# Cross attention with latents: the steps of all engines ordered by due times, and the mask's additive row made on VectorE

## The reference, cut to what matters

```python
x   = _layernorm(features, gm, bm)          # context, 16 x 128 x 256
lat = _layernorm(latents, gl, bl)           # latents, 16 x 128 x 256, normalised once more before this
kv_input = jnp.concatenate([x, lat], axis=1)                      # 256 rows
q, k, v = lat @ Wq, kv_input @ Wk, kv_input @ Wv                  # 16 heads of 64
sim = einsum('bhqd,bhfd->bhqf', q * SCALE, k)
sim = where(kv_mask, sim - max(sim), -inf)                        # mask over the 128 context rows only
out = einsum('bhqf,bhfd->bhqd', softmax(sim), v) @ Wo             # added to the activations
```

## Time and profile before

| what | value |
|---|---|
| median of 3 runs | 4432.84 us (4424.89 to 4438.37) |
| the profiled execution's own time | 4435.27 us |
| its span | 4433.8 us |
| busy over the span | PE 74%, DVE 56%, ACT 37%, POOL 32% |
| the stage | 2047.9 to 2777.9 us, 730 us |
| in the stage (2047 to 2785) | PE busy 602.4 us, DVE 240.8, ACT 258.2, POOL 137.1; mean granted clock 0.96 |

### The profile page before, as it was taken

One profiled execution on the slowest core, in us unless ns is written; L12 is line 12 of the kernel. 1 busy time (PEld: TensorE's weight loads), 2 busy tenths in 40 slices (PEclk: granted clock), 3 DMA queues, 4 the chain that ended last, 5 costly groups with the idle time before them and its releaser, 6 DMA issues. The chain is left out here.

```text
span 4433.8 us, 52962 instructions
## 1 busy us (share of the span) xinstructions
PE 3279.0 (74%) x17693; PEld 2111.6 (48%) x17693; DVE 2479.3 (56%) x6511; ACT 1624.7 (37%) x3647; POOL 1407.1 (32%) x1086
## 2 busy tenths in 40 slices
PE   5988887867925677766888888466679666767698
PEld 3666665646612233223566656345456422335555
DVE  6878784364336888885323323535442278855443
ACT  3666654111204544542333334224302144424311
POOL 4666664103452444452212212200010245520010
PEclk7888887888967888888999999679869778989899
DMA  2000000302430000000000000110021200000000
GB/s 89 5 9 6 9 8 9 124 20 82 127 111 39 0 0 0 0 0 14 7 1 1 1 1 1 37 78 1 13 101 29 74 0 1 0 27 1 1 1 20
DMA packets 71034, 116.12 MB, mean 26 GB/s; under 512 B 28689, under 2 KB 58537, under 8 KB 68018
## 3 DMA queue, kind: packets, MB, share of 16 engines
q1 hardware_dynamic: 61170, 86.50, 5.8%
q0 software_dynamic: 9600, 26.23, 2.4%
HBM read 88.58 MB, written 24.12 MB: 25 GB/s over the span
## 5 line engine op out<-in xcount | busy, mean ns | idle before, releaser
L1224 POOL TENSOR_TENSOR L_attn_state<-L_attn_state,L_attn_ccol 128x1024 f32<-128x1024 f32 x192 | 452.3, 2356 | 527.5 <-DVE L_attn_state L1217 526.1
L1217 DVE TENSOR_TENSOR_SCAN L_attn_state<-L_attn_decay,bank 128x1024 f32<-128x1024 f32 x192 | 438.3, 2283 | 41.1 <-ACT L_attn_decay L1194 15.3
L1183 PE MATMUL bank<-L_attn_state,ident 128*128 128x512 f32 x768 | 421.2, 678 | 19.4 <-POOL L_attn_state L1224 19.3
L1177 PE MATMUL bank<-L_attn_parts,L_attn_select 96*128 96x512 bf16 x384 | 137.9, 441 | 256.7 <-DVE bank L1209 241.8
L1194 ACT ACTIVATE L_attn_decay<-L_attn_dt,L_attn_A 128x512 f32<-128x512 f32 x384 | 256.2, 716 | 129.3 <-DVE L_attn_state L1217 116.3
L1103 POOL TENSOR_TENSOR L_xattn_prob<-L_xattn_prob,L_xattn_inv 128x1024 f32<-128x1024 f32 x64 | 121.2, 1895 | 567.2 <-DVE L_xattn_inv L1086 567.2
L1209 DVE TENSOR_TENSOR bank<-L_attn_dtx,bank 128x1024 f32<-128x1024 f32 x192 | 236.0, 1229 | 57.0 <-PE bank L1177 50.7
L1183 PEld LDWEIGHTS bank<-L_attn_state,ident 128*128 128x128 f32 x768 | 164.7, 217 | 185.4 <-issue 129.9
L1177 PEld LDWEIGHTS bank<-L_attn_parts,L_attn_select 96*128 96x128 bf16 x384 | 29.9, 102 | 391.0 <-DVE bank L1209 340.0
L736 ACT ACTIVATE L_xattn_prob<-bank,L_xattn_top 128x128 f32<-128x128 f32 x512 | 135.8, 416 | 195.9 <-DVE L_xattn_top L778 195.9
L1027 ACT ACTIVATE L_xattn_prob<-L_xattn_masked,L_xattn_low 128x256 f32<-128x256 f32 x256 | 127.0, 497 | 209.2 <-DVE L_xattn_low L1081 127.3
(11 more groups left out here) (601 smaller groups left out, 7705.4 us busy)
## 6 DMA issues: line engine op xcount, KB each, us to landing
L_ffn_ew<-in_L_ffn_experts SPq DMA_DIRECT2D x4, 3072.0 KB, 21.2
L_ffn_made<-L_ffn_yout SPq DMA_DIRECT2D x24, 512.0 KB, 3.0
L_ffn_w<-in_L_ffn_w SPq DMA_DIRECT2D x4, 2048.0 KB, 14.6
L_xattn_ctx<-in_ctx_rows SPq DMA_DIRECT2D x3, 2048.0 KB, 8.2
L_ffn_rows<-L_ffn_xh SPq DMA_DIRECT2D x8, 512.0 KB, 2.9
L_ffn_made<-L_ffn_yout SPq DMA_DIRECT2D x12, 256.0 KB, 2.1
L_attn_rows<-in_x SPq DMA_DIRECT2D x16, 128.0 KB, 6.9
turned<-L_attn_rows SPq DMA_DIRECT2D x16, 128.0 KB, 2.3
```

The costliest lines, as they stand in the source:

```text
L1177: pe.matmul(self.spread.bank(2 * N + i)[:, :], self.select[:, NSTATE * i + n, :], parts[:, :], start=True, stop=True).then_inc(*self.sprea ...
L1183: t = pe.matmul(self.y[unit % len(self.y)][m][:, :], self.c.ident[:, :], self.state[N % 3][:, m, :], start=n == 0, stop=n == 15)
L1217: dve.tensor_tensor_scan(flat(self.state[N % 3]), flat(self.decay[N % 2]), flat(self.drive), 0.0, ALU.mult, ALU.add).then_inc(*self.scanne ...
L1224: pool.tensor_tensor(state[:, :, :], state[:, :, :], self.ccol[N % 2][:, :].unsqueeze(1).broadcast_to([P, 2, GT]), ALU.mult).then_inc(*sel ...
```

## The change

In words:

- The order comes from three tables of due times, in units of a quarter of a sequence: one for steps that come once (or twice) per unit, one for those of a sequence (period 4), one for those of a group of four sequences (period 16). All steps are sorted by their time.
- Filling a bank and copying it out are now steps of their own (q and qcopy, k and kcopy, v and vcopy, flip and flipped, turn and turned, mix and unmix, out and add), so the copy can have another place in its engine's list than the fill in TensorE's.
- low and exp are split by bank (j = 0, 1), with two signals `softened` per unit.
- The norms and the first q and k of sequence 0 are written out in front.
- The mask's weights are loaded onto all 128 partitions (the DMA's source repeats the row). Per sequence one DVE instruction makes `hidden` from them (step hidden). The step hide, its fill of the side bank, its copy, the cast, the tile `hide` and TensorE's wait at the beginning are gone. DVE does the memset of `hidden` alone at the start.
- As copies have places of their own, two waits are new: qcopy waits until the scores of sequence a-2 were filled, and hidden until they were emptied. The banks, what fills them and who empties which are as before.

The core of the diff:

```diff
+LATENTS_BY_UNIT = {"score": -0.06, "low": (-0.06, 0.72), "exp": (0.58, 1.11), "invert": 1.37, "flip": (2.15, 2.29), "flipped": (2.31, 2.4),
+                   "mix": 2.61}
+LATENTS_BY_SEQUENCE = {"turn": -2.96, "turned": -2.96, "q": (-2.57, -1.04), "qcopy": (-2.42, -1.18), "kcopy": (-2.38, -1.34, -0.67, -0.54),
+                       "k": (-2.11, -1.46, -0.78, -0.67), "hidden": -0.49, "vcopy": (-0.37, 0.17, 0.49, 0.81), "v": (-0.35, 0.07, 0.39, 0.64),
+                       "unmix": (4.77, 6.27), "out": 6.63, "add": 6.89}
+LATENTS_BY_GROUP = {"stats_other": -11.44, "stats_outer": -6.96, "apply_outer": -5.74, "apply_other": -4.85, "stats_inner": -3.89,
+                    "apply_inner": -3.38}
...
+def due_by(table, period, turns):
+    for kind, at in table.items():
+        each = at if isinstance(at, tuple) else (at,)
+        yield from ((period * turn + time, kind, len(each) * turn + i) for turn in turns for i, time in enumerate(each))
...
     def order():
         yield "begin", 0
-        yield from norms(0)
-        yield from front(0)
...
+        for step in LATENTS_BY_GROUP:
+            yield step, 0
+        yield "hidden", 0
+        for what, copied, times in (("turn", "turned", 1), ("q", "qcopy", 2), ("k", "kcopy", 4)):
+            for n in range(times):
+                yield what, n
+                yield copied, n
+        first = ("hidden", "turn", "turned", "q", "qcopy", "k", "kcopy")
+        due = chain(due_by(LATENTS_BY_UNIT, 1, range(UNITS)), due_by(LATENTS_BY_SEQUENCE, 4, range(NSEQ)), due_by(LATENTS_BY_GROUP, 16, range(1, NGROUP)))
+        yield from as_due([(time, kind, n) for time, kind, n in due if kind not in first or n >= {"q": 2, "qcopy": 2, "k": 4, "kcopy": 4}.get(kind, 1)])
...
-        elif what == "hide":
-            at = side[what, n]
-            dve.wait_ge(*side.filled(at))
-            dve.tensor_copy(hidden[n % 2][:, 0:P], side.bank(at)[:, 0:P]).then_inc(*side.done(at))
+        elif what == "hidden":
+            if n >= 2:
+                dve.wait_ge(*score[1].emptied(4 * (n - 2) + 3))
+            else:
+                dve.wait_ge(*cleared.at(0))
+            dve.tensor_scalar(hidden[n % 2][:, 0:P], w["keep"][:, n * P:(n + 1) * P], 0.0, 1e30, ALU.is_equal, ALU.mult).then_inc(*hid.up())
...
+        elif what == "exp":
+            i, j = divmod(n, 2)
+            if i >= 3 and j == 0:
+                act.wait_ge(*flip.filled(2 * (i - 3) + 1))
+            act.wait_ge(*score[j].emptied(i))
+            for h in (j, 2 + j):
+                t = act.activation(prob[i % 3][:, h, :], masked[i % 2][:, h, :], ACT.Exp, bias=low[:, i % 2, h:h + 1], scale=-1.0,
+                                   accum_out=total[:, i % 3, h:h + 1])
             t.then_inc(*softened.up())
```

More of the change, by code:

```diff
@@ L52, in __init__ @@
         self.gone = {e: s.flag(f"{name}_emptied_{e}") for e in sorted(set(by))}
+        self.latest = {}
     def bank(self, n):
@@ L837, in order @@
     def order():
[L838 to L843, removed]
-        yield "begin", 0
-        yield from norms(0)
-        yield from front(0)
[L847 to L873, removed]
@@ L1001, in scalar @@
             act.wait_ge(*w.ready)
-        elif what == "turn":
-            at = side[what, n]
+        elif what == "turned":
+            at = side["turn", n]
             act.wait_ge(*side.filled(at))
@@ L1009, in scalar @@
             t.then_inc(*side.done(at))
-        elif what == "q":
+        elif what == "qcopy":
             a, half = divmod(n, 2)
-            at = side[what, n]
+            at = side["q", n]
+            if a >= 2 and half == 0:
+                act.wait_ge(*score[1].filled(4 * (a - 2) + 3))
             act.wait_ge(*side.filled(at))
@@ L1015, in scalar @@
                            scale=-hd ** -0.5).then_inc(*side.done(at))
-        elif what == "k" and n % 2 == 0:
+        elif what == "kcopy" and n % 2 == 0:
             empty_k(act, act.copy, n)
-        elif what == "v" and n % 2 == 1:
+        elif what == "vcopy" and n % 2 == 1:
             empty_v(act, act.copy, n)
[L1020 to L1028, removed]
+        elif what == "exp":
[6 more added lines that the diff above has]
+                                   accum_out=total[:, i % 3, h:h + 1])
             t.then_inc(*softened.up())
-        elif what == "flip" and n % 2 == 0:
+        elif what == "flipped" and n % 2 == 0:
             empty_flip(act, act.copy, n)
-        elif what == "mix" and n % 2:
-            a, pair = divmod(n // 2, 2)
+        elif what == "unmix":
+            a, pair = divmod(n, 2)
             if a >= 2:
                 act.wait_ge(*side.filled(side["out", a - 2]))
-            act.wait_ge(*mixed.at(n))
+            act.wait_ge(*mixed.at(2 * n + 1))
             act.copy(oT[a % 2][:, 4 * pair:4 * pair + 4, :].rearrange("p m t -> p (m t)"), c.banks[6][:, :]).then_inc(*unmixed.up())
@@ L1063, in vector @@
             inner.apply(n, lambda b: u[:, b, :], lambda b: lat[n % 2][:, b, :])
[L1064 to L1068 removed]
+        elif what == "hidden":
[4 more added lines that the diff above has]
+            dve.tensor_scalar(hidden[n % 2][:, 0:P], w["keep"][:, n * P:(n + 1) * P], 0.0, 1e30, ALU.is_equal, ALU.mult).then_inc(*hid.up())
+        elif what == "kcopy" and n % 2:
             empty_k(dve, dve.tensor_copy, n)
[L1070 removed]
+        elif what == "vcopy" and n % 2 == 0:
             empty_v(dve, dve.tensor_copy, n)
[L1072 to L1083, removed]
+        elif what == "low":
+            i, j = divmod(n, 2)
+            if i % 4 == 0 and j == 0:
+                dve.wait_ge(*hid.at(i // 4))
+            if i >= 2:
+                dve.wait_ge(*softened.at(i - 2, j))
+            dve.wait_ge(*score[j].filled(i))
+            for m in range(2):
+                h = 2 * m + j
+                t = dve.tensor_tensor_reduce(masked[i % 2][:, h, :], score[j].bank(i)[:, m * 2 * P:(m + 1) * 2 * P], hidden[i // 4 % 2][:, :], 1.0, 3e38,
+                                             ALU.add, ALU.min, low[:, i % 2, h:h + 1])
+            t.then_inc(*score[j].done(i))
         elif what == "invert":
@@ L1086, in vector @@
             dve.reciprocal(inv[:, n % 3, :], total[:, n % 3, :]).then_inc(*inverted.up())
-        elif what == "flip" and n % 2:
+        elif what == "flipped" and n % 2:
             empty_flip(dve, dve.tensor_copy, n)
-        elif what == "out":
-            at = side[what, n]
+        elif what == "add":
+            at = side["out", n]
             dve.wait_ge(*side.filled(at))
```

31 lines of the change are left out of this document (16 added, 15 removed).

## The result

| | before | after |
|---|---|---|
| median | 4432.99 us (4424.89 to 4438.37, 4 runs) | 4327.28 us (4324.41 to 4332.49, 4 runs) |
| the profiled execution | 4435.27 us | 4328.89 us |
| its stage | 2047.9 to 2777.9, 730.0 us | 2047.5 to 2673.5, 626.0 us |

The ratio is 0.9766 (95% interval 0.9754 to 0.9778): 106 us faster, where 100 had been forecast. 104.0 us of it lie in the stage.

A forecast was written before the change was run, and what follows sets the result against it. TensorE bounds the stage, idling by order ahead of side steps. Turn 1 at 2096.4, first period 35, 13 periods 482.3, norms 1.5 and end 62.5 give 2677.7 against 2777.9: 100 us less, 4333 us, range 4314 to 4380.

The forecast's parts named there:

- The walk: Engines' lists followed through one middle sequence: 35.7 us of TensorE work plus 1.4 idle, 37.1 us in place of 43.8.
- The norms: Next group's norms on DVE land where it has at least 1.2 us to spare; 0.5 us per group, 1.5 in all.
- The start: Stage's beginning: context statistics come first and wait for DMA, turn starts 2.3 us later, turn 1 at 2096.4 against 2095.9.
- The end: From the last sequence's turn to the stage's end: 62.5 us in place of 69.1.
- hide goes: Mask step off TensorE: per sequence 0.41 us of PE and one trip, 0.89 us idle, are removed.
- hidden at 0.3 us, nobody waits: DVE's tensor_scalar making the mask's row takes near 0.3 us, bounded by 0.2 and 0.57, and holds nobody up.
- The order: TensorE's sorted list puts 1.02 us or more of work behind all side steps but three, covering trips of 0.68 to 0.78.
- Rival A: Order gains half: real lists slip against the plan, periods reach only 39.9 us; 4372 us, chance 0.18.
- Rival B: Slower: q, k and v copies stuck behind exps in ACT's list, 15.6 us more a sequence; 4558 us, chance 0.04.
- Rival C: No change: TensorE's idle comes from a clock or limit, so denser work gets less clock; 4433 us, chance 0.04.
- rival D: Better than walked: time at the lower clock and the open 1.4 us vanish, 20 us less; 4313 us, chance 0.06.
- Rival E: Mask row's tensor_scalar on DVE and POOL's multiplication exclude each other in SBUF, 30 us over forecast; 4363 us, chance 0.03.

The follow-up runs named there:

- hide put back: Kernel after the change with the hide step, its fill, VectorE copy and the cast restored just ahead of turn: ratio 0.9809 to before, stage 643.1 us.
- late exps alone: Kernel before, with low, exp and invert moved to the end of each unit's list, TensorE's order and hide kept: ratio 0.9976 to before, stage 722 us.
- late exps with the mask's edit: Kernel before, with low, exp and invert at the end of each unit's list and the mask's row made on VectorE: ratio 0.9921, stage 696.2 us.
- whole early units: Kernel after, with low and exp of a unit unsplit and right behind its score, copies keeping their own places: ratio 0.9993 to before, stage 729.8 us.
- mask alone: Kernel before, in its old order, with only the mask's row made on VectorE and no hide fill: ratio 1.0039 to before, stage 744.0 us.

## Why the prediction was right, point by point

- **What bounds it.** Right: PE, idle ahead of side steps, by order. The stage is PE's work of 35.5 us a sequence plus 1.2 idle, forecast 35.7 plus 1.4.
- **The walk.** 36.7 us a sequence, and 37.1 with norms, for 37.1 and 0.5 more. The open places are the three that it named, with 0.72, 0.25 and 0.24 for 0.7, 0.3 and 0.3. From turn 2 to turn 15 that makes 478.6 us for 483.8, so this term was 5.2 us too long.
- **The norms.** "Each lands where DVE has at least 1.2 us to spare" is wrong in one place: the flip copy behind a norm comes late and a mix waits 0.28 us. The price was right in kind, 0.34 us a group for 0.5.
- **The start.** Turn 0 came as forecast (15.9 us into the stage, forecast 16.3). What failed is "the next fills follow one by one as before": three fills in a row at the lower clock made it 35.7 us to turn 1 for 32.2 forecast. The first period was shorter in turn, 32.8 for 35.
- **The end.** 63.0 us, forecast 62.5.
- **How the terms meet.** Turn 1 was 2.8 us late, the first period 2.2 us shorter, the thirteen periods with norms 5.2 shorter, the end 0.5 longer: the stage ended 4.2 us before the forecast. The closeness is in part luck, as the start's error and the first period's nearly cancel.
- **hide goes.** "Per sequence 0.41 us of PE and one trip (0.89 us idle) are removed" is right beside the new order (1.24 us by the run with hide put back) and wrong beside the old one, where it lay in the exps' shadow. The sum had it in the new order only, so the time was right.
- **hidden at 0.3 us, nobody waits.** 0.22 us, and nobody did.
- **The order.** The text names two causes, that a flip "covers only 0.5" of a trip (TensorE's list) and that a copy "stands behind the unit's four exps in ACT's list", and prices them only together. The price was right. What it did not see is that neither works alone, and that an exp ahead of a copy costs its own wait for low (1.46 us) as well as its length. Against the kernel before, TensorE's list with the mask's edit brings nothing, late exps alone 8 us, late exps with the mask's edit 34, and all together 104.
- **Rival A** (39.9 us at best) fell: no period from turn 1 on was above 37.1 us.
- **Rival B** had the right mechanism and the right place. The run with whole early units is that rival in part: 6.2 us of pauses a sequence, and it ends at the time of before, not above.
- **Rival C** (denser work gets less clock): the contrary, the clock rose from 0.97 to 1.00 in the middle of the stage. That is about 20 us of the gain. No term of the sum had it apart: the 37.1 us were added up from durations at the full clock, so the forecast took it for granted that the clock would hold. For the same reason the first half of rival D ("the time at the lower clock falls away too") had no price left.
- **Rival E** did not come about: hidden took 0.22 us in all 16 sequences.
- **Outside the stage** 2.4 us of the 106.4 between the two profiled executions; not explained, and within what executions differ by.

## What to carry to other kernels

When several engines walk one list in strict order, look at each engine's list for an instruction that waits for work only just begun, with a copy behind it that TensorE wants: its wait counts as well as its length. Put such a chain later (here by about a half unit, and in two halves), look at what it then stands ahead of on the other engines (here invert, on VectorE), and change TensorE's order with it. Judge single edits only with the others in place, since each uncovers the next wait. Then count the steps that need cover against the pieces that can give it; a walk through one period, from durations of the trace, was right to 1%.

## What the runs showed of the hardware that I had not expected

- How often the q behind turn ran at the lower clock goes neither by the longest pause ahead of it nor by the pauses' sum. With a single pause of 0.72 us it never did. With 1.7 us ahead of turn and 0.7 to 1.2 behind it (late exps) it did in 10 of 10 sequences, with a single 2.71 (late exps and mask) in 4 of 10, with 0.9 and 2.05 (before) in 7 of 11, with a single 3.06 to 3.8 (whole early) in 8 of 15 and only in part, with a single 3.57 to 3.9 (mask alone) in 11 of 12, and there also with 2.55 to 2.69 in 3 of 3. The q then takes up to 3.79 us for 2.05, and the mix behind it up to 1.98 for 1.09. What decides it stays open. Removing work from such a place made the kernel slower.
- A VectorE instruction of 0.2 us takes 1.55 when a multiplication on GpSimd is under way, and ends 0.1 us behind it.
